# Spreading the inverted softmax sums over the rows: DMAs through memory in place of matmuls, and the normalisation one step later

## The chip, the cores and the metric

The kernel runs on one core of one Trainium2 chip. The metric is device time in microseconds (us): the median of the runs. A profile of one execution stands beside it. The core has TensorE (PE; its weight loads are PEld), VectorE (DVE), ScalarE (ACT), GpSimd (POOL) and SyncE (SP), which here only issues DMAs.

## The reference, cut to what matters

A block of a transformer: cross-attention with a gate, then a mixture of 8 experts with a gate. Only the attention is touched.

```python
x: (4, 512, 512)        # 4 batches of 512 tokens
q = ln(x) @ Wq.T + bq   # 16 heads of 32
k, v = ctx @ Wk.T + bk, ctx @ Wv.T + bv          # 64 context tokens
scores = clip(q k / sqrt(32), -50, 50), masked
probs = softmax(scores)                           # over the 64 context tokens
ctx = einsum(probs, v)                            # 512 tokens x (16 heads x 32)
delta = rs * (ctx @ Wo.T + bo);  x = x + tanh(g) * layernorm(delta) * gamma + beta
x = x + tanh(g2) * experts(ln(x))                 # top 2 of 8
```

The kernel divides by the softmax sum after the product with v: `o_un` is the sum over exp(score) times v, and it is multiplied by the inverse of the sum of its head and token.

## The kernel before, in words

Everything of the attention is kept with features on the partitions and the 512 tokens of a batch along the free axis. The 512 features of a head product are four chunks m (KC = 4) of 128 partitions, and a chunk holds 4 heads a of 32 features. The sums `den` and their inverse `rden` are 16 x 512 (a row per head), so each row must reach the 32 partitions of its head.

Products are made in three fp32r matmuls of a high and a low part (`product3`, L241 to L247; all these matmuls carry line L245). So each operand is split: ACT writes the high part, and DVE or POOL writes the low part, the value minus the high part.

The program is written out by hand for each engine, with semaphores between them. A batch (`batch(b, back, front)`) has 9 steps s = 0 to 8; a step makes the scores of one pair of heads, clips them (DVE), takes their exponential and its two halves (ACT, POOL: `ex_lo`) and multiplies by v (`pv`, one step later). `back` means that the work of the batch before is interleaved: normalising its `o_un`, its output product (`o_product(b - 1, t)` in steps 2 to 5, one tile t of 128 tokens each), its layer norm and update (`update_and_residual`), and the router. `front` means that the next batch is prepared: statistics of its x in steps 1 and 2 (DVE), transposes in step 4, the first half of its q. Batches 1 and 2 have both; batch 0 has no back, batch 3 no front. A tail after batch 3 does the back part of batch 3 alone, and the routing and 37 expert slots follow.

The way of the inverse before: at the end of a batch ACT copies `den` (L946); DVE inverts it (`invert_sums`, L386 to L392) and splits the inverse into `r_hi` and `r_lo`. In step 0 of the next batch PE multiplies both by a selection matrix `bsel` of 16 x 128 for each chunk (`spread`, L1101 to L1111), chunks 0 and 1 behind the q product of chunk 2, and chunks 2 and 3 behind that of chunk 3. DVE multiplies the result in PSUM by `o_un` into `o_n` (two buffers; `normalise`, L394 to L399), ACT copies that to `o_hi` (L899), and POOL subtracts to `o_lo` (L737; in the tail DVE does it, L539). `o_product(n, 0)` waits for each of the four `o_lo` chunks as it comes to it (L1118).

SP issues, in order: for a batch with front the load of the next x into `xs` (L290); with back the stores of the updated rows as they come (L282, L284); then the load of this batch's rows again for the residual, `xr` (L295). The statistics of x wait for `xs` at L346.

Of the kernel before, what the change touches and what calls it, by code (L numbers as in the profile page):

```python
# [41 lines left out]
def flamingo_gated_block(nc, x, ctx_t, mask, w_attn, b_cols, b_rows, gates, gate_t, w_exp, out):  # L42
    st = ExitStack()
    with st:
# [10 lines left out]
        pad_cw = h_dram.rearrange("(n p) d -> n p d", p=P)[NT][:, H:HW]  # L55
        out_rows = out.rearrange("(n p) d -> n p d", p=P)
# [67 lines left out]
        o_n = sb("o_n", [P, 2, S], F32, pa)  # L124
# [76 lines left out]
        def f32(ap):  # L201
            return ap.bitcast(F32)
# [16 lines left out]
        pair_mm, o_ev, den_c, den_r, r_h, r_l, r_mm, o_nd, o_h, o_l = (sem(n) for n in  # L219
            ("pair_product", "context_copied", "sums_copied", "sums_inverted", "inverse_hi", "inverse_lo",  # L220
# [47 lines left out]
        def _(sp):  # L268
# [17 lines left out]
            def batch(b, back, front):  # L286
# [8 lines left out]
                sp.dma_start(xr[:, :, :], x_b[b]).then_inc(rload, 16)  # L295

# [34 lines left out]
        def _(dve):  # L331
# [54 lines left out]
            def invert_sums(n):  # L386
                dve.wait_ge(den_c, n + 1)
                dve.reciprocal(rden[:, :], den[:, :]).then_inc(den_r, 1)  # L388
                dve.wait_ge(den_r, n + 1)
                dve.tensor_scalar(r_hi[:, :], rden[:, :], 1.0, None, ALU.mult).then_inc(r_h, 1)  # L390
                dve.wait_ge(r_h, n + 1)
                dve.tensor_tensor(r_lo[:, :], rden[:, :], f32(r_hi[:, :]), ALU.subtract).then_inc(r_l, 1)  # L392

            def normalise(n, m):  # L394
                dve.wait_ge(r_mm, n * KC + m + 1)
                dve.wait_ge(o_ev, n * KC + m + 1)
                if m >= 2:
                    dve.wait_ge(o_l, n * KC + m - 1)
                dve.tensor_tensor(o_n[:, m % 2, :], bank[m % 2][:, :], o_un[:, m, :], ALU.mult).then_inc(o_nd, 1)  # L399
# [47 lines left out]
            def batch(b, back, front):  # L447
                for s in range(PAIRS + 1):
# [86 lines left out]
            for m in range(KC):  # L535
# [3 lines left out]
                dve.tensor_tensor(o_lo[:, m, :], o_n[:, m % 2, :], f32(o_hi[:, m, :]), ALU.subtract).then_inc(o_l, 1)  # L539
# [165 lines left out]
        def _(pool):  # L705
# [7 lines left out]
            pool.memset(rden[:, :], 1.0).then_inc(setup, 1)  # L713
# [631 lines left out]
```

## Time and profile before

| | us |
|---|---|
| median of 3 runs | 1033.14 |
| lowest and highest | 1032.68, 1034.61 |
| the profiled execution: its span (no other time is listed for it) | 1037.1 |
| PE busy | 929.8 (90%) |
| DVE busy | 471.1 (45%) |
| ACT busy | 366.3 (35%) |
| POOL busy | 261.1 (25%) |
| granted TensorE clock, mean | 0.947 |

The attention with its tail takes the first 290 us or so: setup and projections to about 49, batch 0 to 84, batch 1 to 137, batch 2 to 192, batch 3 to 246, and the tail. A profile row gives the start and duration in us, the engine and the source line, the operation with output and inputs, the shapes and the count. What stands in square brackets is the idle time of the engine just before, and who ended it. The busy share of PE is not PE at its peak, because matmuls overlap: in a chain at full clock a matmul of 512 columns is listed with 0.39 us but starts 0.23 us after the one before.

### The profile page before, as it was taken

Reading aid. Unit: us, or ns where it says so; the run is one execution under the profiler, and the core shown is the slowest. Engines: PE = TensorE matmul, PEld = TensorE weight load, DVE = VectorE, ACT = ScalarE, POOL = GpSimd, SP = SyncE. Lnnn points to the kernel's source line nnn. Section 1 sums busy time; section 2 is a strip of 40 time slices with the busy share of each in tenths; the row PEclk is TensorE's granted clock in tenths of the full one; section 3 lists DMA queues with packets and bytes.
Section 4 is the critical chain, followed back from the end, with each engine's and each line's share of the span. In section 5 each row is a group of like instructions: output and inputs, shape, how many; then the busy total and the mean of one; then the engine's idle time right before and its main releaser. Section 6 shows DMA issues by size and latency. Waiting matters only on the chain.

```text
span 1037.1 us, 14215 instructions
## 1 busy us (share of the span) xinstructions
PE 929.8 (90%) x4201; PEld 723.2 (70%) x4202; DVE 471.1 (45%) x796; ACT 366.3 (35%) x663; POOL 261.1 (25%) x283
## 2 busy tenths in 40 slices
PE   3989999996719999989989989989989998999994
PEld 3756767674517888768868868768868877888883
DVE  5648978786776221451351451621351244226311
ACT  3455554523203222432432442522432253226221
POOL 4034545363231211211211211211211112113111
PEclk9989989997858999999999999999999999999997
DMA  7020121212626211351351361621261235212121
GB/s 289 30 93 0 72 91 51 71 51 77 238 95 253 30 31 30 107 186 30 95 199 28 90 206 26 219 80 22 69 233 20 41 101 182 36 25 30 31 30 20
DMA packets 27824, 93.65 MB, mean 90 GB/s; under 512 B 5408, under 2 KB 5408, under 8 KB 21024
## 3 DMA queue, kind: packets, MB, share of 16 engines
q1 hardware_dynamic: 18528, 72.03, 19.1%
q0 software_dynamic: 8560, 20.35, 10.5%
q10 hardware_dynamic: 720, 1.07, 0.3%
q8 instruction: 8, 0.13, 0.1%
q14 instruction: 8, 0.07, 0.0%
HBM read 74.76 MB, written 18.68 MB: 90 GB/s over the span
## 4 chain that ended last, share of the span: by engine, by line
PE 61%; DMA 16%; issue 9%; DVE 5%; POOL 4%; ACT 2%; POOLq 0%; SPq 0%; DVEq 0%; ACTq 0%
PE bank L245 53%; DMA xg<-h_rows,g_idx 8%; DMA out_rows<-y_sb,s_idx 7%; PE bank L1270 2%; PE bank L1257 2%; DMA xs<-in_x 2%; POOL s_idx L840 1%; PE bank L1143 1%; DVE rden L388 1%; DVE xr L408 1%; ACT y_sb L1045 1%; PE bank L1097 1%; PE bank L1109 1%; PE bank L1130 1%; PE bank L1061 1%
## 5 line engine op out<-in xcount | busy, mean ns | idle before, releaser
L245 PE MATMUL bank<-g_hi,gt_hi 128*128 128x512 f32 x592 | 237.7, 402 | 1.6 <-DVE gt_lo L656 1.6
L245 PE MATMUL bank<-g_hi,gt_lo 128*128 128x512 f32 x592 | 234.7, 396 | 0.0
L245 PE MATMUL bank<-g_lo,gt_hi 128*128 128x512 f32 x592 | 234.5, 396 | 0.0
L686 DVE TENSOR_TENSOR hid<-silu,bank 128x256 f32<-128x256 f32 x148 | 61.5, 420 | 316.6 <-ACT silu L1026 316.5
L1026 ACT ACTIVATE silu<-bank 128x256 f32<-128x256 f32 x148 | 56.7, 383 | 253.2 <-PE bank L245 253.2
L245 PEld LDWEIGHTS bank<-g_hi,gt_hi 128*128 128x128 f32 x592 | 111.7, 189 | 27.6 <-issue 2.0
L245 PEld LDWEIGHTS bank<-g_hi,gt_lo 128*128 128x128 f32 x592 | 111.5, 188 | 27.2
L245 PE MATMUL bank<-dn_hi,hd_hi 128*128 128x512 f32 x296 | 130.2, 440 | 0.0
L245 PEld LDWEIGHTS bank<-g_lo,gt_hi 128*128 128x128 f32 x592 | 111.8, 189 | 25.8
L245 PE MATMUL bank<-dn_lo,hd_hi 128*128 128x512 f32 x296 | 120.0, 405 | 0.0
L245 PE MATMUL bank<-dn_hi,hd_lo 128*128 128x512 f32 x296 | 119.2, 403 | 0.0
L840 POOL COPY s_idx<-slot_idx 128x1 int32 x37 | 20.3, 548 | 357.3 <-ACT y_sb L1045 357.3
L549 DVE TENSOR_TENSOR g_lo<-raw,g_hi 128x2048 fp32r<-128x2048 f32 x32 | 72.4, 2286 | 9.8 <-ACT g_hi L975 9.7
L669 DVE TENSOR_TENSOR hd_lo<-bank,hd_hi 128x256 fp32r<-128x256 f32 x148 | 58.9, 419 | 35.8 <-ACT hd_hi L1009 35.8
L245 PEld LDWEIGHTS bank<-dn_hi,hd_lo 128*128 128x128 f32 x296 | 57.6, 194 | 14.4
L1009 ACT ACTIVATE hd_hi<-bank 128x256 fp32r<-128x256 f32 x148 | 52.5, 384 | 41.4 <-PE bank L1270 41.4
L843 POOL DMA_INDIRECT out_rows<-y_sb,s_idx x37 | 59.3, 1602 | 30.1 <-POOL s_idx L840 30.1
L698 DVE TENSOR_TENSOR gt_lo<-bank,gt_hi 128x512 fp32r<-128x512 f32 x37 | 25.6, 692 | 88.3 <-ACT gt_hi L1038 88.3
L756 POOL TENSOR_TENSOR ex_lo<-ex,ex_hi 128x512 fp32r<-128x512 f32 x32 | 42.0, 1312 | 91.8 <-ACT ex_hi L922 91.7
L975 ACT ACTIVATE g_hi<-raw 128x2048 fp32r<-128x2048 f32 x32 | 61.1, 1910 | 10.5 <-PE bank L245 10.5
L245 PEld LDWEIGHTS bank<-dn_lo,hd_hi 128*128 128x128 f32 x296 | 58.2, 197 | 8.9
L245 PEld LDWEIGHTS bank<-dn_hi,hd_hi 128*128 128x128 f32 x296 | 57.9, 196 | 9.1
(215 smaller groups left out, 1317.4 us busy)
## 6 DMA issues: line engine op xcount, KB each, us to landing
raw<-in_w_exp SPq DMA_DIRECT2D x48, 1024.0 KB, 6.4
raw<-in_w_attn SPq DMA_DIRECT2D x4, 1024.0 KB, 13.6
xs<-in_x SPq DMA_DIRECT2D x4, 1024.0 KB, 6.5
xr<-in_x SPq DMA_DIRECT2D x4, 1024.0 KB, 5.9
out_rows<-xr SPq DMA_DIRECT2D x16, 256.0 KB, 2.0
h_rows<-dh SPq DMA_DIRECT2D x16, 256.0 KB, 2.1
rows<-in_b_rows ACTq DMA_DIRECT2D x1, 1024.0 KB, 13.3
c_raw<-in_ctx_t SPq DMA_DIRECT2D x1, 640.0 KB, 4.2
```

What stands on the lines that cost most here:

```text
L245: mm = eng.matmul(psum, a(k), b(k), start=(first and k == 0 and j == 0), stop=(last and k == n - 1 and j == 2))
L549: dve.tensor_tensor(dst.rearrange("p k n -> p (k n)"), raw[:, p, :], f32(hi.rearrange("p k n -> p (k n)")), ALU.subtract).then_inc(done, 1)
L669: dve.tensor_tensor(hd_lo[:, 2 * p:2 * p + 2, :].rearrange("p k n -> p (k n)"), bank[4 + p % 2][:, 0:256], f32(hd_hi[:, 2 * p:2 * p + 2, : ...
L686: dve.tensor_tensor(hid[:, p, :], silu[:, p, :], bank[p][:, 256:512], ALU.mult).then_inc(hid_done, 1)
L698: dve.tensor_tensor(gt_lo[:, :, :].rearrange("p k n -> p (k n)"), bank[6][:, :], f32(gt_hi[:, :, :].rearrange("p k n -> p (k n)")), ALU.su ...
L756: pool.tensor_tensor(ex_lo[:, s % 2, :], ex[:, s % 2, :], f32(ex_hi[:, s % 2, :]), ALU.subtract).then_inc(e_l, 1)
L840: pool.tensor_copy(s_idx[:, :], slot_idx[:, bass.ds(g, 1)]).then_inc(idx_s, 1)
L843: pool.indirect_dma_start(out=out[:, :], out_offset=bass.IndirectOffsetOnAxis(ap=s_idx[:, 0:1], axis=0), in_=y_sb[:, :], in_offset=None, c ...
L975: act.activation(dst.rearrange("p k n -> p (k n)"), raw[:, p, :], ACT.Copy).then_inc(done, 1)
L1009: act.activation(hd_hi[:, 2 * p:2 * p + 2, :].rearrange("p k n -> p (k n)"), bank[4 + p % 2][:, 0:256], ACT.Copy).then_inc(hd_h, 1)
L1026: act.activation(silu[:, p, :], bank[p][:, 0:256], ACT.Silu).then_inc(silu_done, 1)
L1257: tr = pe.transpose(bank[6][:, k * P:(k + 1) * P], xg[:, k * P:(k + 1) * P], ident[:, :])
```

## The change

The inverse is no longer split and multiplied by `bsel`. A scratch tensor in DRAM, `inverse_rows` (16 x 512), takes `rden` in one store of 32 KB; then four loads, one for each head a of the chunks, read it back, each with a broadcast over 32 partitions and all four chunks m, into a new tile `rbc` (128 x 4 x 512, 1024 KB in all). SP issues all five, after the load of `xr`, and waits for the inverse, for the last `o_lo` of the batch before (which reads `rbc`) and then for its own store. `normalise` multiplies `rbc` by `o_un` in place; `o_hi` and `o_lo` read `rbc` in place of `o_n`. In a batch, the four normalisations, `o_hi` and `o_lo` move from step 0 to step 1. `bsel`, `r_hi`, `r_lo`, `o_n`, `spread`, and the setup of `bsel` are gone.

```diff
+        r_dram = nc.dram_tensor("inverse_rows", [NH, S], F32).ap()
+        r_spread = r_dram.rearrange("(m a) s -> a m s", a=4)
...
-        bsel = sb("bsel", [NH, KC, 4, HD], F32R, pa)
-        r_hi = sb("r_hi", [NH, S], F32R, pa)
-        r_lo = sb("r_lo", [NH, S], F32R, pa)
+        rbc = sb("rbc", [P, KC, S], F32, pa)
-        o_n = sb("o_n", [P, 2, S], F32, pa)
...
 # SP, end of batch
                 sp.dma_start(xr[:, :, :], x_b[b]).then_inc(rload, 16)
+                sp.wait_ge(den_r, b + 1)
+                if back:
+                    sp.wait_ge(o_l, b * KC)
+                sp.dma_start(r_dram, rden[:, :]).then_inc(r_out, 16)
+                sp.wait_ge(r_out, b * 16 + 16)
+                for a in range(4):
+                    sp.dma_start(rbc[a * HD:a * HD + HD, :, :], r_spread[a].partition_broadcast(HD)).then_inc(r_in, 16)
...
 # DVE
             def invert_sums(n):
                 dve.wait_ge(den_c, n + 1)
                 dve.reciprocal(rden[:, :], den[:, :]).then_inc(den_r, 1)
-                dve.wait_ge(den_r, n + 1)
-                dve.tensor_scalar(r_hi[:, :], rden[:, :], 1.0, None, ALU.mult).then_inc(r_h, 1)
-                dve.wait_ge(r_h, n + 1)
-                dve.tensor_tensor(r_lo[:, :], rden[:, :], f32(r_hi[:, :]), ALU.subtract).then_inc(r_l, 1)

             def normalise(n, m):
-                dve.wait_ge(r_mm, n * KC + m + 1)
+                if m == 0:
+                    dve.wait_ge(r_in, n * 64 + 64)
                 dve.wait_ge(o_ev, n * KC + m + 1)
-                if m >= 2:
-                    dve.wait_ge(o_l, n * KC + m - 1)
-                dve.tensor_tensor(o_n[:, m % 2, :], bank[m % 2][:, :], o_un[:, m, :], ALU.mult).then_inc(o_nd, 1)
+                dve.tensor_tensor(rbc[:, m, :], rbc[:, m, :], o_un[:, m, :], ALU.mult).then_inc(o_nd, 1)
...
                     if s == 0:
-                        if back:
-                            normalise(b - 1, 0)
-                            normalise(b - 1, 1)
                         q_low(b, 2)
                         if back:
                             v_low(b)
-                            normalise(b - 1, 2)
-                            normalise(b - 1, 3)
                         q_low(b, 3)
+                    if s == 1 and back:
+                        for m in range(KC):
+                            normalise(b - 1, m)
...
 # POOL: setup of bsel (a memset of rden, an affine select) gone; o_low in step 1
-                    if s == 0 and back:
+                    if s == 1 and back:
                         for m in range(KC):
                             o_low(b - 1, m)
...
 # ACT: the four o_high in step 1, behind the exponential
+                    if s == 1 and back:
+                        for m in range(KC):
+                            o_high(b - 1, m)
...
 # PE, step 0
                         q_product(b, 2)
-                        if back:
-                            spread(b - 1, 0)
-                            spread(b - 1, 1)
                         pe.wait_ge(q_l, b * KC + 2)
                         q_product(b, 3)
-                        if back:
-                            spread(b - 1, 2)
-                            spread(b - 1, 3)
...
 # PE, tail
-            for m in range(KC):
-                spread(NB - 1, m)
```

## Rows read from the trace of the kernel before

**Rows 1.** Stretches: length, busy (count) of PE, PEld, DVE, ACT, POOL, clock, DMA share, GB/s.

```profile
84.00:95.00 11.00, 10.06 (x38) 6.62 (x38) 10.57 (x12) 5.29 (x11) 3.90 (x3) 1.00 0.00 0
...
150.00:165.00 15.00, 15.00 (x50) 10.24 (x49) 12.71 (x28) 7.78 (x12) 11.44 (x11) 0.80 0.05 17
165.00:194.00 29.00, 29.00 (x151) 20.88 (x150) 23.02 (x46) 15.36 (x30) 12.41 (x13) 1.00 0.29 99
...
246.00:249.00 3.00, 0.00 (x0) 0.00 (x0) 3.00 (x1) 0.00 (x0) 2.96 (x3) 0.88 0.00 0
...
255.00:258.00 3.00, 3.00 (x7) 1.90 (x7) 2.71 (x5) 1.41 (x3) 0.00 (x0) 0.50 0.00 0
258.00:261.00 3.00, 3.00 (x13) 2.42 (x12) 1.51 (x3) 0.04 (x1) 0.00 (x0) 0.92 0.86 276
```

**Rows 2.** Timeline, DVE's inversions at the end of batches 0 to 3.

```profile
84.16 3.34 DVE L388 RECIPROCAL rden<-den 16x512 f32<-16x512 f32 x1
...
137.41 3.34 DVE L388 RECIPROCAL rden<-den 16x512 f32<-16x512 f32 x1
...
192.57 3.34 DVE L388 RECIPROCAL rden<-den 16x512 f32<-16x512 f32 x1
...
245.70 3.33 DVE L388 RECIPROCAL rden<-den 16x512 f32<-16x512 f32 x1
```

**Rows 3.** Timeline of the tail, from the inverse to the output product.

```profile
246.03 5.10 POOL L741 TENSOR_TENSOR xr<-xr,rows 128x512 f32<-128x512 f32 x4 [4.25 <-DMA xr<-in_x]
250.05 1.63 DVE L392 TENSOR_TENSOR r_lo<-rden,r_hi 16x512 fp32r<-16x512 f32 x1
251.73 0.79 PE L1109 MATMUL bank<-r_hi,bsel 16*128 16x512 f32 x1 [6.28 <-DVE r_lo L392]
252.98 0.69 DVE L399 TENSOR_TENSOR o_n<-bank,o_un 128x512 f32<-128x512 f32 x1 [1.31 <-PE bank L1109]
253.71 0.63 ACT L899 ACTIVATE o_hi<-o_n 128x512 fp32r<-128x512 f32 x1 [8.12 <-DVE o_n L399]
254.44 0.68 DVE L539 TENSOR_TENSOR o_lo<-o_n,o_hi 128x512 fp32r<-128x512 f32 x1
...
255.73 0.80 PE L245 MATMUL bank<-w_hi,o_hi 128*128 128x512 f32 x1
...
257.40 0.82 SPq L306 DMA_DIRECT2D raw<-in_w_exp  x2
...
260.15 0.75 DVE L415 SCALAR_TENSOR_TENSOR dh<-bank,tg,rows 128x512 f32<-128x512 f32 x1 [1.39 <-PE bank L245]
```

**Rows 4.** Timeline, what follows the first output product in batches 1, 2 and 3.

```profile
100.58 0.50 PE L245 MATMUL bank<-ex_hi,vbd_hi 128*128 128x512 f32 x1
101.79 0.74 DVE L415 SCALAR_TENSOR_TENSOR dh<-bank,tg,rows 128x512 f32<-128x512 f32 x1
...
156.84 0.39 PE L245 MATMUL bank<-ex_hi,vbd_hi 128*128 128x512 f32 x1
157.11 0.75 DVE L415 SCALAR_TENSOR_TENSOR dh<-bank,tg,rows 128x512 f32<-128x512 f32 x1 [1.86 <-PE bank L245]
...
212.03 0.75 DVE L415 SCALAR_TENSOR_TENSOR dh<-bank,tg,rows 128x512 f32<-128x512 f32 x1 [3.81 <-PE bank L245]
```

**Rows 5.** By tile: duration min, median, max in ns, first and last start.

```profile
L1109 PE MATMUL bank<-r_hi,bsel x16: 384/490/790, 88.8 to 254.7; 16*128 16x512 f32 x16
...
L737 POOL TENSOR_TENSOR o_lo<-o_n,o_hi x12: 1278/1314/1362, 92.1 to 206.2; 128x512 fp32r<-128x512 f32 x12
```

**Rows 6.** GB/s of 60 to 70; DMA issues (KB, us to landing) of 128 to 140, 105 to 125.

```profile
GB/s 0 0 0 0 0 0 0 0 0 33 0 0 0 0 0 0 49 164 41 115 270 328 393 418 377 426 410 393 401 279 82 33 16 0 0 0 0 66 0 0
...
xr<-in_x SPq DMA_DIRECT2D x1, 1024.0 KB, 5.8
xs<-in_x SPq DMA_DIRECT2D x1, 1024.0 KB, 7.5
...
out_rows<-xr SPq DMA_DIRECT2D x3, 256.0 KB, 2.0
```

More of the change, by code:

```diff
@@ L218, in flamingo_gated_block @@
             ("scores_product", "scores_clipped", "exp_done", "exp_hi_done", "exp_lo_done"))
-        pair_mm, o_ev, den_c, den_r, r_h, r_l, r_mm, o_nd, o_h, o_l = (sem(n) for n in
-            ("pair_product", "context_copied", "sums_copied", "sums_inverted", "inverse_hi", "inverse_lo",
+        pair_mm, o_ev, den_c, den_r, r_out, r_in, o_nd, o_h, o_l = (sem(n) for n in
+            ("pair_product", "context_copied", "sums_copied", "sums_inverted", "inverse_stored",
              "inverse_spread", "context_normalised", "o_hi_done", "o_lo_done"))
@@ L538, in _ @@
                 dve.wait_ge(o_h, (NB - 1) * KC + m + 1)
-                dve.tensor_tensor(o_lo[:, m, :], o_n[:, m % 2, :], f32(o_hi[:, m, :]), ALU.subtract).then_inc(o_l, 1)
+                dve.tensor_tensor(o_lo[:, m, :], rbc[:, m, :], f32(o_hi[:, m, :]), ALU.subtract).then_inc(o_l, 1)
             for t in range(TT + 2):
@@ L712, in _ @@
                 pool.memset(f32(tile[:]), 0.0).then_inc(setup, 1)
-            pool.memset(rden[:, :], 1.0).then_inc(setup, 1)
-            pool.wait_ge(setup, 9)
+            pool.wait_ge(setup, 8)
             for g in range(2):
                 pool.memset(f32(hsel[g * T:g * T + T, NH - 2 + g:NH - 1 + g]), 1.0).then_inc(setup, 1)
-            pool.affine_select(out=bsel[:, :, :, :], in_=rden[:, :].rearrange("p (m a d) -> p m a d", m=KC, a=4),
-                               compare_op=ALU.is_equal,
-                               fill=0.0, base=0, pattern=[[-4, KC], [-1, 4], [0, HD]],
-                               channel_multiplier=1).then_inc(setup, 1)
             pool.dma_start(out_rows[NT], f32(kbd_hi[:, :, :]).rearrange("p k n -> p (k n)")).then_inc(pad_store, 16)
@@ L736, in o_low @@
                 pool.wait_ge(o_h, n * KC + m + 1)
-                pool.tensor_tensor(o_lo[:, m, :], o_n[:, m % 2, :], f32(o_hi[:, m, :]), ALU.subtract).then_inc(o_l, 1)
+                pool.tensor_tensor(o_lo[:, m, :], rbc[:, m, :], f32(o_hi[:, m, :]), ALU.subtract).then_inc(o_l, 1)
             def add_beta(n, t):
@@ L768, in batch @@
                         add_beta(b - 1, s - 1)
-            pool.wait_ge(setup, 12)
+            pool.wait_ge(setup, 10)
             ln_inverse(0)
@@ L898, in o_high @@
                 act.wait_ge(o_nd, n * KC + m + 1)
-                act.activation(o_hi[:, m, :], o_n[:, m % 2, :], ACT.Copy).then_inc(o_h, 1)
+                act.activation(o_hi[:, m, :], rbc[:, m, :], ACT.Copy).then_inc(o_h, 1)
             def h_copy(n, t, tail=False):
@@ L958, in _ @@
             x_high(0, range(2, KC))
-            act.wait_ge(setup, 12)
+            act.wait_ge(setup, 10)
             act.wait_ge(pad_store, 48)
@@ L1052, in _ @@
             pe.sem_inc(y_ready, 1)
-            pe.wait_ge(setup, 12)
+            pe.wait_ge(setup, 10)
             def x_transposes(n, chunks=range(KC)):
@@ L1099, in pv @@
                 mm.then_inc(pair_mm, 1)
-            def spread(n, m):
-                if m == 0:
-                    pe.wait_ge(r_l, n + 1)
-                    pe.wait_ge(lg_done, n * TT + TT)
-                if m >= 2:
-                    pe.wait_ge(o_nd, n * KC + m - 1)
-                for a, r_ in enumerate((r_hi, r_lo)):
-                    mm = pe.matmul(bank[m % 2][:, :], bsel[:, m, :, :].rearrange("p a d -> p (a d)"), r_[:, :],
-                                   start=(a == 0), stop=(a == 1))
-                mm.then_inc(r_mm, 1)
             def o_product(n, t):
```

6 lines of the change are left out of this document (removed).

## Prediction

> **What bounds the kernel now.** I read first the busy time and clock by stretch, then the timeline around the end of each batch, then the DMA answers. The change sits only in the attention stage and its tail, up to some 290 us; the 37 expert slots behind it keep their work and simply start later or earlier. In the stretch 165 to 194 PE is busy all 29 us at clock 1.00, and in 150 to 165 it is busy all 15 us but at clock 0.80 [rows 1]: inside a batch TensorE sets the pace, and a piece of it runs at 1.2 instead of 2.4 GHz. The start of a batch is different: 84 to 95 has 0.9 us without PE. The reader is to see that whatever delays PE in steps 0 to 2 of a batch is paid nearly in full, because no idle PE time follows in which to win it back. DVE is close behind: it starts `dh` for tile 0 as soon as the first output product is ready, at 101.79, 157.11 and 212.03 us, the last two after 1.9 and 3.8 us of waiting for PE [rows 4]. In batch 3 and in the tail this DVE/POOL chain (scale, statistics, power, update) is the bound, and it starts from the same product. So in all four places one event counts: the end of `o_product(0)`, which needs all four `o_lo` chunks.
>
> The clock: the first spread of the tail starts at 251.73 after 6.28 us of idle, so PE's work ended at 245.45; the clock is 0.88 on the mean of 246 to 249, so it fell near 248.3, some 3 us later; it is 0.50 in 255 to 258 and 0.92 in 258 to 261 [rows 1, 3]. It came back about 6.5 us after work resumed. I use these two as observed, at every gap.
>
> **What is removed.** Per batch 8 matmuls for `spread`, 0.38 to 0.49 us each and overlapping [rows 5], at most 3.1 to 3.9 us of PE, plus PE's wait for `r_lo` in front of them; and the two DVE instructions `r_hi` and `r_lo`. This shortens the time from the inverse to the end of step 0 by about 3 us in batches 1 to 3. It is worth money only if PE is then what ends the wait for `o_product(0)`; below it is not. In the setup, POOL loses one memset and one select; PE starts behind the first split of a weight, long after POOL's setup, so this is nothing, and could only be a gain.
>
> **What is added: a round trip.** The inverse is ready 3.34 us after its start, at 87.50, 140.75, 195.91 and 249.03 [rows 2]. From there: SP wakes and issues, for which I allow 0.17 us without a row. The store of 32 KB: the 256 KB stores land after 2.0 us [rows 6]; most of that can hardly be the bytes, so I take 2.0 for the small one at both ends. Another 0.17 us. Then four loads of 256 KB, each to 32 partitions. Low end: each lands like a lone 256 KB store, 2.0 us, and the last is issued 3 x 0.41 = 1.2 us after the first (two issues in 0.82 us [rows 3]): 3.2 us. Nearest row: the 1024 KB load of x, the same bytes, 5.8 us just before another load [rows 6]. High end: the data part of that load, some 2.6 us near 400 GB/s [rows 6], takes twice as long: 8.4 us. I take the row, 5.8, plus 1.2 us, since the last quarter of the bytes is only issued then: 7.0. The round trip is 0.17 + 2.0 + 0.17 + 7.0 = 9.3 us (ends 5.5 and 10.7).
>
> `rbc` is complete at 96.8, 150.1, 205.2 and 258.3.
>
> **Behind the round trip, in a batch.** The wait stands on DVE at step 1, and queued behind it are the statistics of the next x and the clip of step 2; for that clip wait ACT's exponential, POOL's `ex_lo` and `pv(2)`, and behind the moved `o_hi` and `o_lo` the same two stand in their own queues. All of that is needed only after `o_product(0)` and `pv(1)`, so the product is late first. One normalise (0.69 us) and one `o_hi` (0.63) with hand-overs, as the tail shows (252.98, 253.71, 254.44: 1.46 us for both) [rows 3], take 1.5 us; then POOL does four `o_lo` of 1.31 us [rows 5], 5.3 us; the remaining normalises and `o_hi` pass beside them. The normalise reads two SBUF tiles now, where one came from PSUM. Such a DVE instruction waits for a POOL instruction in progress: `r_lo`, 0.68 us otherwise, took 1.63 beside POOL's `xr` [rows 3]. Two of the four meet this, +0.6 to 1.0 us each; the fourth is then normalised about 3.7 us after the landing, POOL asks for it after 5.4. Cover: 1.7 us minus `o_hi`. The last three matmuls of `o_product(0)` follow, 0.43 us apart (512 columns at 1.2 GHz; 12 of them 5.1 us). Sum: landing + 1.5 + 5.3 + 1.3 = landing + 8.1.
>
> Batch 1: 104.9, where the following matmul group started at 100.58 and DVE at 101.79 [rows 4]: PE +4.3, DVE +3.2. PE idles more than 4 us ahead of the first chunk, so the clock falls here, where it was 1.00 before [rows 1], and comes back near 105; the next 5 matmuls lose up to 1 us. I take +4.5.
> Batch 2: 158.2 against 156.84 and 157.11 [rows 4]: PE +1.4 plus up to 0.9 of slow clock, DVE +1.2. I take +1.8. The 3 us saved on PE and the slow clock of before (0.80 in 150 to 165) are why it is less than in batch 1.
> Batch 3: 213.3 against 212.03 (DVE is the bound): +1.4.
> Tail: landing 258.3, normalise, `o_hi` and DVE's `o_lo` at 0.73 us each, PE starts at 260.6 instead of 255.73 [rows 3]: +4.9. Before, the spread matmuls had run since 251.73 and the clock was back 2.7 us into the output product; now it starts cold and all 12 matmuls of tile 0 take 5.1 us instead of 4.4: +0.8. Together +5.7, all of it on the chain that `dh` at 260.15 begins.
> Sum: 4.5 + 1.8 + 1.4 + 5.7 = 13.4 us.
>
> **What is moved.** The load of the next x is issued behind the four spread loads; before, it went out a step or more ahead of the batch's end. SP waits in order for `den_r` and the store. In batches 1 and 2 DVE wants it right after the fourth normalise, about landing + 3.7. It lands after the spreads: two loads issued one behind the other took 5.8 and 7.5 us [rows 6], so the second comes some 2.6 us behind the first: landing + 2.6. It is hidden with 1.1 us to spare. Were that cover gone, each microsecond would stop DVE's clip of step 2 twice. The load of the residual and the stores of the batch are issued ahead of the wait or well after it: nothing. In the tail the first expert weights wait for the last normalise as before, and are wanted only when the output product is done: nothing. `o_un` is not overwritten before the normalises: its next copy is behind two `pv` steps; nothing, with some microseconds of cover.
>
> **A rule of the Trainium skill.** The row: loads to 128 partitions move near 400 GB/s for 2.6 us [rows 6]; none of this size goes to 32. "SBUF — State Buffer", section "Door 1: The DMA port swizzle", says that the transfer rate depends on how many of 16 ports the partitions reach, that 32 partitions reach 8 of them, and that two transfers at once do not add up. By its 189 GB/s (estimate, that page) the megabyte takes 5.5 us of data instead of 2.6, and the sum would be some 25 us instead of 13. The rule speaks against this change; it is the first rival.
>
> **Rivals.**
> (1) Half rate for the four loads: 8.4 us plus part of the issue lag, 1.4 to 2.4 us more than I took. No row speaks against it; for it, each load touches a quarter of the partitions and all of them read the same 32 KB. It counts in all four places at full: 4 x 1.4 to 4 x 2.4, +19 to +23 us, and x lands late as well, up to 1 us in two batches. Some 1054 us.
> (2) The other side: the quarters overlap, round trip 5.5 us or less. Then `rbc` is there at 93.0, 146.3, 201.4 and 254.5; the clock holds, and `o_product(0)` ends at landing + 7.5: batch 1 0, batch 2 about -2.8, batch 3 -2.9 (the removed matmuls pay at last), tail +1.9: -3.8, 1029 us. It turns at a round trip of about 6.4 us. For it: a lone 256 KB transfer takes 2.0. Against it: 1 MB took 5.8 us.
> (3) The round trip is as I say but x ends the wait of DVE in batches 1 and 2 by 2 us or more, as its one landing of 7.5 us could stretch with the spreads ahead of it: +4, 1050 us.
>
> **How the numbers follow.** The profiled execution spans 1037.1 us and nothing else of it is listed; the median of the runs is 1033.1, 0.4% less. I add the difference to the median: 1033.1 + 13.4 = 1046.5, say 1046. The own range of the forecast is 1040 to 1051 (a round trip of 7.8 to 10.5). Chances: forecast 0.58, rival 1 0.22, rival 2 0.12, rival 3 0.08. The range reaches from 1037 to 1056: it leaves out most of rival 2 and the far part of rival 1. A measurement of this kernel tells 0.2%, 2 us, from no change. Faster by more: 0.08, from rival 2; within: 0.04, its slow edge; slower: 0.88.
>
> **What would show it.** Right: PE idle in front of the first `w_hi,o_hi` matmul in each batch, released by `o_lo`; DVE waiting for the DMA of `rbc` 8 to 10 us after the inverse; half clock at the start of the output product in batch 1 too; `dh` of tile 0 in the tail 17 us after the inverse instead of 11.1 [rows 2, 3]. Wrong: a landing under 6 us after the inverse; PE released by `q_lo` or the probabilities rather than by `o_lo`; a wait of DVE for `xs`; or a later stretch of a batch that gives back what its start lost, which would make the mechanism right and the sum too large.

## The result, and the profile after

The changed kernel takes 1044.61 us (median of 4 runs, 1043.32 to 1047.95) against 1033.88 us for the kernel before on the same chip (4 runs, 1032.68 to 1037.04): ratio 1.0100, 95% interval 1.0065 to 1.0135. Run again unedited later (`changed_again`, 6 runs) it took 1045.84 against 1034.85: ratio 1.0101, interval 1.0068 to 1.0133. It is 10.7 to 11.0 us slower.

First the timeline of the changed kernel around the start of batch 1; it answers to [rows 2, 4]. SPq rows are the issues of DMAs, with the time that SP spent on them.

```profile
79.73 3.34 DVE L394 RECIPROCAL rden<-den 16x512 f32<-16x512 f32 x1
...
83.10 0.34 SPq L298 DMA_DIRECT2D inverse_rows<-rden  x1
...
84.70 1.75 SPq L301 DMA_DIRECT2D rbc<-inverse_rows  x4
...
86.82 0.41 SPq L289 DMA_DIRECT2D xs<-in_x  x1
...
92.85 3.58 DVE L400 TENSOR_TENSOR rbc<-rbc,o_un 128x512 f32<-128x512 f32 x4 [4.00 <-DMA rbc<-inverse_rows]
...
94.28 5.81 POOL L730 TENSOR_TENSOR o_lo<-rbc,o_hi 128x512 fp32r<-128x512 f32 x4 [2.77 <-ACT o_hi L892]
...
95.93 0.79 PE L244 MATMUL bank<-w_hi,o_hi 128*128 128x512 f32 x1 [6.14 <-POOL o_lo L730]
...
101.27 0.74 DVE L416 SCALAR_TENSOR_TENSOR dh<-bank,tg,rows 128x512 f32<-128x512 f32 x1
```

Read it as a chain. The inverse ends at 83.07. The store is issued at once and has landed 1.6 us later, when SP issues the loads; these occupy SP for 1.75 us, and DVE, idle for 4.00 us, starts when they have landed, at 92.85: 8.15 us after the first was issued and 9.78 us after the inverse. POOL then does its four `o_lo` in 5.81 us, 1.45 each, and PE, idle for 6.14 us, waits for them chunk by chunk. The other three places repeat it; each shows the inverse, DVE's first normalise and `dh` of tile 0:

```profile
136.89 3.34 DVE L394 RECIPROCAL rden<-den 16x512 f32<-16x512 f32 x1
...
149.22 3.58 DVE L400 TENSOR_TENSOR rbc<-rbc,o_un 128x512 f32<-128x512 f32 x4 [3.74 <-DMA rbc<-inverse_rows]
...
158.06 0.75 DVE L416 SCALAR_TENSOR_TENSOR dh<-bank,tg,rows 128x512 f32<-128x512 f32 x1 [0.32 <-PE bank L244]
...
193.68 3.34 DVE L394 RECIPROCAL rden<-den 16x512 f32<-16x512 f32 x1
...
205.70 3.58 DVE L400 TENSOR_TENSOR rbc<-rbc,o_un 128x512 f32<-128x512 f32 x4 [3.46 <-DMA rbc<-inverse_rows]
...
214.07 0.75 DVE L416 SCALAR_TENSOR_TENSOR dh<-bank,tg,rows 128x512 f32<-128x512 f32 x1 [4.12 <-PE bank L244]
...
247.73 3.33 DVE L394 RECIPROCAL rden<-den 16x512 f32<-16x512 f32 x1
...
260.01 1.29 DVE L400 TENSOR_TENSOR rbc<-rbc,o_un 128x512 f32<-128x512 f32 x2 [8.95 <-DMA rbc<-inverse_rows]
...
262.15 0.80 PE L244 MATMUL bank<-w_hi,o_hi 128*128 128x512 f32 x1 [14.66 <-DVE o_lo L538]
...
267.38 0.75 DVE L416 SCALAR_TENSOR_TENSOR dh<-bank,tg,rows 128x512 f32<-128x512 f32 x1 [2.09 <-PE bank L244]
```

From the start of an inverse to `dh` of tile 0 these rows give 21.54, 21.17, 20.39 and 19.65 us. Before they were 17.63, 19.70, 19.46 and 14.45 [rows 2 to 4]. The difference is 3.9 + 1.5 + 0.9 + 5.2 = 11.5 us, and the medians differ by 10.7. Within the attention nothing gives it back: from inverse to inverse the batches are longer by 3.9, 1.6 and 0.9 us (57.16, 56.79 and 54.05 against 53.25, 55.16 and 53.13). The two profiled spans differ by less, 1041.6 against 1037.1: the profiled run of before spent 4.4 us more ahead of its first inverse (84.16 against 79.73), and 2.8 us more behind `dh` of the tail (777.0 against 774.2). That last stretch varies from 772.8 to 779.0 us over all the profiles here, so a small gain in the expert stage is neither shown nor excluded.

The stretches from the inverse to `dh` in both kernels show the clock. First the kernel before, batches 1, 2 and 3 (columns as in [rows 1]):

```profile
84.20:101.80 17.60, 16.49 (x63) 10.97 (x63) 17.04 (x27) 8.86 (x17) 9.03 (x8) 1.00 0.00 0
137.40:157.10 19.70, 17.93 (x59) 11.98 (x59) 17.37 (x26) 8.37 (x16) 10.92 (x9) 0.83 0.01 4
192.60:212.00 19.40, 17.86 (x59) 11.99 (x58) 13.96 (x16) 8.35 (x15) 10.20 (x8) 0.82 0.00 0
```

The changed kernel, the same three, then the wait of the tail and the start of its output product:

```profile
79.70:101.30 21.60, 15.08 (x52) 10.07 (x53) 16.52 (x26) 9.01 (x17) 9.57 (x8) 0.84 0.40 99
136.90:158.10 21.20, 15.00 (x51) 10.14 (x50) 16.65 (x25) 8.48 (x16) 9.99 (x8) 0.84 0.36 100
193.70:214.10 20.40, 14.37 (x51) 9.52 (x50) 12.47 (x15) 8.45 (x15) 9.52 (x7) 0.83 0.24 53
249.00:262.00 13.00, 0.00 (x0) 0.00 (x0) 3.95 (x4) 1.23 (x2) 3.44 (x3) 0.53 0.38 84
...
262.00:266.00 4.00, 3.85 (x9) 2.96 (x10) 3.19 (x6) 1.26 (x2) 0.00 (x0) 0.50 0.27 55
```

Batch 1 has gone from 1.00 to 0.84; batches 2 and 3 were at 0.83 and 0.82 already. So batch 1 was the one that ran quickly before (17.63 us, against 19.70 and 19.46), and its loss is the largest for that; after the change all three take 20.4 to 21.5. The fall of the clock in the changed kernel is not itself the price: `fill_wait` below keeps it at 1.00, and batch 1 still takes 21.50. The DMAs of 84 to 105 us answer to [rows 6]:

```profile
rbc<-inverse_rows SPq DMA_DIRECT2D x4, 256.0 KB, 5.3
xs<-in_x SPq DMA_DIRECT2D x1, 1024.0 KB, 8.5
```

The x load, issued at 86.82, landed at 95.3. DVE was normalising until 96.4 and never waited for it.

### The profile page after: what moved, and what is told of

The parts are those of the page before. It is cut to its first block, busy times and chain, and to the rows that moved or that the text cites. A ratio compares the mean times of both kernels' runs of the same rounds, so it can differ in the third digit from the quotient of the medians.

```text
span 1041.6 us, 14150 instructions
## 1 busy us (share of the span) xinstructions
PE 912.7 (88%) x4169; PEld 712.8 (68%) x4170; DVE 465.2 (45%) x788; ACT 366.3 (35%) x663; POOL 261.1 (25%) x281
## 4 chain that ended last, share of the span: by engine, by line
PE 56%; DMA 18%; issue 11%; DVE 5%; POOL 5%; ACT 3%; POOLq 0%; SPq 0%; DVEq 0%; ACTq 0%
PE bank L244 49%; DMA xg<-h_rows,g_idx 8%; DMA out_rows<-y_sb,s_idx 7%; PE bank L1240 2%; PE bank L1227 2%; DMA xs<-in_x 2%; POOL s_idx L833 1%; POOL o_lo L730 1%; DMA rbc<-inverse_rows 1%; DVE xr L409 1%; ACT y_sb L1035 1%; POOL ex_lo L749 1%; PE bank L1121 1%; DVE st L424 1%; DVE rden L394 1%
```

## The experiments

The table sets beside each other, for every kernel, the median, its ratio to the kernel before with the interval, and the time from the start of the inverse to `dh` of tile 0 in batches 1, 2, 3 and the tail (from the timeline of its one profile). The kernel before had medians of 1033.58 to 1034.85 in the four sets of runs beside these.

| kernel | us | ratio (95%) | b1 | b2 | b3 | tail |
|---|---|---|---|---|---|---|
| before | 1033.88 | | 17.63 | 19.70 | 19.46 | 14.45 |
| changed | 1044.61 | 1.0100 (1.0065 to 1.0135) | 21.54 | 21.17 | 20.39 | 19.65 |
| changed_again | 1045.84 | 1.0101 (1.0068 to 1.0133) | 22.12 | 21.16 | 20.49 | 19.65 |
| store_twice | 1051.09 | 1.0154 (1.0119 to 1.0189) | 22.13 | 22.15 | 22.23 | 20.69 |
| two_queues | 1048.45 | 1.0134 (1.0097 to 1.0172) | 21.32 | 22.28 | 21.63 | 17.73 |
| tail_matmul_2 | 1042.59 | 1.0072 (1.0049 to 1.0094) | 22.23 | 21.61 | 20.44 | 15.47 |
| move_only | 1036.95 | 1.0031 (1.0005 to 1.0057) | 20.09 | 20.23 | 19.28 | 14.18 |
| fill_wait | 1046.59 | 1.0111 (1.0074 to 1.0147) | 21.50 | 20.71 | 20.53 | 18.36 |
| eight_back | 1048.67 | 1.0143 (1.0114 to 1.0171) | 21.75 | 21.31 | 21.81 | 19.61 |
| before_warm_tail | 1029.71 | 0.9956 (0.9930 to 0.9983) | 17.62 | 17.79 | 19.46 | 13.66 |
| warm_again | 1034.17 | 1.0001 (0.9974 to 1.0028) | 17.66 | 19.71 | 19.47 | 13.63 |
| warm_only | 1032.41 | 0.9983 (0.9954 to 1.0012) | 18.83 | 17.77 | 17.59 | 15.32 |
| pool_wait_only | 1035.42 | 1.0013 (0.9986 to 1.0040) | 17.65 | 19.69 | 19.46 | 14.20 |

**What sets the time of the loads: probe.** The kernel before, with transfers one after another at its very end, when nothing else runs (one execution; the edit is shown shortened).

```diff
+            sp.dma_start(p_dram, raw[0:NH, 0, 0:S])     # 32 KB store, then wait
+            for a in range(4): quarter(sp, a, spread_src, pr_s[1])   # as in the change
+            for a in range(4): quarter(sp, a, rows_src, pr_s[2])     # distinct rows of x
+            sp.dma_start(t4, x_b[0])                                 # 128 partitions at once
+            sp.dma_start(t4, p_spread[0].partition_broadcast(P))     # 128 partitions, the same 4 rows
```

> The kernel before, and behind its end, when nothing else runs, SP issues transfers one group after the other, each awaited, all with 1024 KB in or out of one tile except where said: a 32 KB store of 16 rows; four quarters to 32 partitions each from the 16 rows just stored (the change's loads); four quarters to the same partitions from distinct rows of x; one load of x to 128 partitions; one load to 128 partitions in which all partitions read the same 4 rows; the four quarters from the 16 rows in the order 0, 2, 1, 3; a single quarter; the store again. Theory A (a transfer to 32 partitions has half the rate, by the partitions it reaches): the quarters of x take as long as those of the stored rows, 7.2 us from the first issue, at about 220 GB/s; both loads to 128 partitions take 5.5 us at up to 400 GB/s; the order 0, 2, 1, 3 gains little. Theory B (the many reads of the same 32 KB in memory are what is slow): the quarters of x take about 5.5 to 6 us, and the load of 128 partitions that read the same 4 rows is slow, 7 us or more. Theory C (four issues instead of one): the quarters of x take 6 to 6.5 us and both loads to 128 partitions 5.5. The store takes 1.6 us in every theory.

Issues in the timeline of `probe`; each group waits for the landing of the one before, so the distance to the next row is the time to landing (the last `x5` are two groups: four quarters in the order 0, 2, 1, 3, and at 1062.48 a lone one):

```profile
1026.44 0.34 SPq L335 DMA_DIRECT2D probe_rows<-raw  x1
...
1028.04 1.76 SPq L340 DMA_DIRECT2D raw<-probe_rows  x4
...
1035.29 1.75 SPq L340 DMA_DIRECT2D raw<-in_x  x4
...
1042.14 0.40 SPq L353 DMA_DIRECT2D raw<-in_x  x1
...
1047.31 0.39 SPq L355 DMA_DIRECT2D raw<-probe_rows  x1
...
1055.56 7.22 SPq L340 DMA_DIRECT2D raw<-probe_rows  x5
```

The store 1.60 us; four quarters from the stored rows 7.25; four quarters of distinct rows 6.85; the same megabyte in one load to 128 partitions 5.17; one load to 128 partitions that all read the same four rows 8.25. In the order 0, 2, 1, 3 the quarters take 6.9. So it is the quarters that cost, 1.7 us over a whole load, and rereading the same rows adds 0.4 to them. Issuing in four pieces is not the cause: a lone quarter lands after 3.4 us, and the last is issued 1.3 us behind the first, which would make 4.7. And one load that reads the same rows for all partitions is the slowest of the four. Theory A is right for the quarters and wrong for that load, theory B the other way round. The rate in 40 equal slices of 1026 to 1060 us shows it from another side:

```profile
GB/s 0 39 0 82 195 282 222 227 166 60 0 0 164 306 193 222 205 145 0 0 87 219 400 402 125 0 125 171 130 176 108 171 176 152 24 14 176 299 236 248
```

After the store (39) come the four transfers, with zeros between: the quarters of stored rows at some 220 GB/s, those of x at some 210, the load to 128 partitions at 400, the one of repeated rows at 108 to 176. The Trainium skill, "SBUF — State Buffer", section "Door 1: The DMA port swizzle", has 32 partitions at 189 GB/s and 128 at 328, both for a whole transfer of 1 MiB, with limits of some 218 and 436 for large ones. The trace agrees with the limits (220 and 210, 400). The prediction took the 189 for the rate of the data alone; at the 220 measured the megabyte is 4.8 us of data and not 5.5.

That transfers to different partitions don't add up, as the prediction has it from the same page, is not borne out by these traces as it stands. With a queue of SP and one of ACT, to partitions 0 to 63 and 64 to 127, the loads of `two_queues` (below) reached 377 GB/s over their best microsecond in the tail, the first row here, and 361 in batch 3. On one queue the best microsecond of four quarters is 318, in the probe's quarters of x, the second row:

```profile
259.70:260.70 1.00, 0.00 (x0) 0.00 (x0) 0.00 (x0) 0.00 (x0) 0.00 (x0) 0.50 1.09 377
...
1036.80:1037.80 1.00, 0.00 (x0) 0.00 (x0) 0.00 (x0) 0.00 (x0) 0.00 (x0) 0.50 1.05 318
```

**Is the round trip on the path: store_twice.** A second store of the same 32 KB between the first and the loads.

```diff
-                sp.wait_ge(r_out, b * 16 + 16)
+                sp.wait_ge(r_out, b * 32 + 16)
+                sp.dma_start(r_dram, rden[:, :]).then_inc(r_out, 16)
+                sp.wait_ge(r_out, b * 32 + 32)
```

> The changed kernel, but SP stores the inverse twice, waiting in between, so that each of the four round trips is 1.6 to 1.8 us longer and nothing else changes. Theory of the prediction (every microsecond of the round trip is paid in all four places, about one for one): 4 x 1.7 = +6 to +7.5 us, 1051 to 1052. Rival (later steps of a batch give back what its start lost, so that only the tail pays): +2 us, 1046 to 1047.

The second store took 1.57 to 1.60 us each time (in batch 2 issued at 147.24, the loads at 148.82). The kernel took 1051.09 us, 6.5 more than the changed one, and 6.0 to 6.2 when each is set against the kernel before in its own set of runs; 4 x 1.58 is 6.3, and the rival said 2. The profiles say less, and not the same in each place: `dh` is 0.6, 1.0, 1.8 and 1.0 us later after the inverse than in the changed kernel, and 5.0 us from the first inverse to `dh` of the tail (4.4 against `changed_again`, whose batch 1 is as long as this one). So most of a longer round trip is paid, in the batches as in the tail; that it is paid in full in every place is not shown.

**Can the round trip be shortened: two_queues.** Two of the four loads are issued by ACT at the end of its batch.

```diff
-                for a in range(4):
+                for a in (0, 1):
...
+            def spread_loads(b):                     # ACT, last in its batch
+                act.wait_ge(r_out, b * 16 + 16)
+                for a in (2, 3):
+                    act.dma_start(rbc[a * HD:a * HD + HD, :, :], ...).then_inc(r_in, 16)
```

> The changed kernel, but the loads of quarters 2 and 3 (partitions 64 to 127) are issued by ACT on its own queue, behind its last work of the batch, while SP issues quarters 0 and 1 (partitions 0 to 63). Theory A (half the SBUF side is used at a time): with both halves in flight at once the spread lands about 1.5 to 2.5 us earlier, so each of the four places gives back that much, 6 to 8 us in all: 1037 to 1039 us. Theory B (the reads of the same 32 KB are slow) or a limit that concurrent transfers share: the landing stays within 0.5 us, and the time within 2 us of the changed kernel, or a little above it for ACT's wait at the start of a batch.

Neither theory was right: the loads landed 6.0 to 6.9 us after the first issue in place of 7.1 to 8.2, the tail gained 1.9 us by it, and the whole became slower. The batches gained nothing, as batch 2 of `two_queues` shows:

```profile
146.65 1.26 POOL L749 TENSOR_TENSOR ex_lo<-ex,ex_hi 128x512 fp32r<-128x512 f32 x1 [13.94 <-ACT ex_hi L920]
...
150.07 4.66 DVE L400 TENSOR_TENSOR rbc<-rbc,o_un 128x512 f32<-128x512 f32 x4 [0.25 <-DMA rbc<-inverse_rows]
...
151.22 1.27 POOL L749 TENSOR_TENSOR ex_lo<-ex,ex_hi 128x512 fp32r<-128x512 f32 x1 [3.31 <-ACT ex_hi L920]
```

The loads are there 0.8 us sooner after the inverse (138.53 to 150.07, 11.5 us, against 12.3), and DVE waits 0.25 us for them instead of 3.74: it has only just got there. ACT's wait for the store holds up what is queued behind it, its exponential, and so POOL's `ex_lo`, PE and DVE's clip. `ex_lo` of the next step now falls on the normalises, which take 4.66 us for four in place of 3.58, and POOL comes to its first `o_lo` 2.4 us after the first normalise starts (152.46) instead of 1.4. A wait had changed its place. By the profile the batches are 2.7 us longer in sum, inverse to inverse, and the tail is 1.9 shorter. The medians differ by 3.8, but the six runs fall in two groups, 1044.7 to 1046.1 and 1050.8 to 1051.9, and the profile is of the fastest; what the second group does more is open.

**How much belongs to the tail: tail_matmul_2.** The changed kernel with the matmul way for batch 3 alone (inverse split in two, `spread` and `normalise` from PSUM in the tail; no store and loads). The two halves lie in `ex_hi` and `ex_lo`: as tiles of their own (`tail_matmul`) they do not fit in SBUF beside `rbc`, the last tile needing 8192 bytes a partition where 6240 are left.

```diff
+                if not front:
+                    return                            # SP: no round trip in batch 3
...
+                if tail:
+                    dve.tensor_scalar(ex_hi[0:NH, 0, :], rden[:, :], 1.0, None, ALU.mult).then_inc(r_h, 1)
...
+                    dve.tensor_tensor(ex_lo[0:NH, 0, :], rden[:, :], f32(ex_hi[0:NH, 0, :]), ALU.subtract).then_inc(r_l, 1)
...
+            for m in range(KC):
+                spread(NB - 1, m)                     # PE, tail
```

> The changed kernel, but batch 3's inverse is spread by the matmuls of before (with bsel, and the two halves kept in ex_hi and ex_lo), in the tail only; batches 0 to 2 keep the DMAs. Theory of the prediction (each round trip is paid where it stands): the tail gets back what it lost, 5 us on the profile between the inverse and the first dh, so 1039 to 1040 us; what is left above the kernel before, 6 us, is the three batches. Rival (the tail's loss is hidden by the load and split of the first expert weights, and the expert stage only starts when those are there): within 1.5 us of the changed kernel.

Median 1042.59, 8.2 us above before, where the changed kernel is 10.7 to 11.0. The tail's time is 15.47 against 19.65 in the profile: 4.2 us there, 2.5 to 2.8 by the medians, whose intervals overlap; 5 was expected, and at most 1.5 by the rival. PE starts the output product 9.87 us after the inverse began, as early as before (10.03). What is not won back, 1.0 us against the 14.45 of before, is the clock: from that matmul to `dh` it is 5.60 us here at 0.50 nearly throughout, and 4.42 before. So the tail's share of the loss is a quarter of it by the medians and up to 5.2 of 11.7 us by the profiles; the larger part lies in the three batches.

**How much belongs to the move: move_only.** The kernel before with `spread`, `normalise`, `o_hi` and `o_lo` in step 1, in PE's, DVE's, ACT's and POOL's order; no DMA.

```diff
-                        if back:
-                            spread(b - 1, 0)
-                            spread(b - 1, 1)
...
+                    if s == 1 and back:
+                        spread(b - 1, 0)
+                        spread(b - 1, 1)
...
+                    if s == 1 and back:
+                        for m in range(KC):
+                            normalise(b - 1, m)
```

> The kernel before with the move alone: spread stays on PE, but stands in step 1 (chunks 0 and 1 behind the scores, 2 and 3 behind pv(0)), and the normalisations, o_hi and o_lo stand in step 1 too. Theory 1 (the round trip alone makes the loss): the move costs little, 1033 to 1036 us; o_lo is still the last thing before o_product(0), now some 2 to 3 us later after the inverse than before, but PE reaches the step earlier. Theory 2 (a good part of the loss in the batches is the move, which puts four o_lo of POOL, 5.3 us, in one row in front of o_product(0)): 1038 us or more.

1036.95 against 1034.35: +2.6 us, interval 0.5 to 5.9, between the two theories. The profile has +2.5 in batch 1, +0.5 in batch 2, -0.2 in batch 3 and -0.3 in the tail, +2.5 in sum: nearly all of it in batch 1. There it is the clock. First PE's output product in batch 1 of the kernel before, then the same of `move_only`, and two stretches of `move_only`:

```profile
97.49 0.50 PE L245 MATMUL bank<-w_hi,o_hi 128*128 128x512 f32 x1
97.83 0.39 PE L245 MATMUL bank<-w_lo,o_hi 128*128 128x512 f32 x1
...
94.15 0.76 PE L245 MATMUL bank<-w_hi,o_hi 128*128 128x512 f32 x1 [0.28 <-POOL o_lo L735]
94.71 0.63 PE L245 MATMUL bank<-w_lo,o_hi 128*128 128x512 f32 x1
...
88.00:91.30 3.30, 3.15 (x12) 1.81 (x11) 3.23 (x5) 1.17 (x2) 0.47 (x1) 1.00 0.00 0
94.30:97.30 3.00, 3.00 (x7) 1.96 (x8) 2.44 (x5) 1.26 (x2) 2.69 (x3) 0.50 0.00 0
```

The product starts 13.62 us after the inverse began, against 13.33 before, but its matmuls follow each other every 0.43 us instead of 0.23, and twelve of them make up the 2.5 us. The clock had fallen near 91.3, though by the profile PE had been idle for only 0.2 us since 80.5; why it fell is open. Batches 2 and 3 are at 0.83 and 0.82 with the move as they are without it, and change by 0.5 and -0.2. So the place in the order costs little by itself. The 2.5 us is no part of the changed kernel's loss in batch 1 either, since with its clock held at 1.00 (`fill_wait`, next) that batch is as long.

**Is it the cold clock: fill_wait.** The changed kernel with 26 matmuls of 512 columns put into PE's wait in step 1, and 62 into that of the tail; their result is read by nobody.

```diff
+                    if s == 1 and back:
+                        fill(b - 1, 26)
...
+            fill(NB - 1, 62)
```

> The changed kernel with matmuls that nobody reads in PE's waits: 26 of 512 columns behind pv(0) of batches 1 to 3, and 62 in front of the tail's output product (6 and 14 us at full clock, about the waits that the profile shows). Everything else is unchanged. Theory 1 (part of the loss is the slow clock after each wait): the output product starts at full clock; in a batch the last three matmuls save 0.6 us and the next group up to 1, in the tail 2 us or so: 1040 to 1042. Theory 2 (the POOL and DMA chain is all): within 1 us of the changed kernel, 1044 to 1046; or slower, if the matmuls run at the slow clock and push the output product back.

The clock stayed at full speed, as the stretches 140 to 160 and 262 to 270 of `fill_wait` show:

```profile
140.00:160.00 20.00, 18.43 (x74) 13.23 (x74) 15.84 (x24) 8.23 (x15) 9.19 (x7) 1.00 0.39 107
...
262.00:270.00 8.00, 7.63 (x32) 5.56 (x31) 5.86 (x10) 2.50 (x4) 0.00 (x0) 1.00 0.29 88
```

The product starts as early as without the filling (16.16 us after the inverse began in batch 1, against 16.20). Only the tail gained clearly, 1.3 us, and batch 2 by 0.5; the median is 1046.59, no better than the changed kernel, as theory 2 has it. In a batch the product is fed by POOL, a chunk every 1.45 us, which is longer than its three matmuls take at either level (3 x 0.43 = 1.3). So in the batches of the changed kernel the slow clock is a companion of the wait and hardly a cost of its own. In the kernel before, where PE itself is what `dh` waits for, it is one: 1.9 us a batch, as `before_warm_tail` shows below.

**Were the removed matmuls worth nothing: eight_back.** The changed kernel with eight matmuls where the spreads stood, beside `changed_again`.

```diff
                         q_product(b, 2)
+                        if back:
+                            fill(b - 1, 4)
...
                         q_product(b, 3)
+                        if back:
+                            fill(b - 1, 4)
```

> The changed kernel with eight matmuls of 128x512 put back into step 0 of each batch with a back part (four behind each of the two q products, where the spreads stood), on operands that are already there; their result is read by nobody, so the output is the same. The prediction held that the eight removed matmuls were worth nothing, since the end of o_product(0) hangs on the round trip and not on PE. That theory expects 1043 to 1046 us, within 2 us of the changed kernel run beside it, PE's idle time ahead of the first output product shorter by about 3 us (from 6.1 us to about 3 in batch 1) and the time from the inverse to dh of tile 0 the same to 0.5 us. The rival, that the removed matmuls gave back up to 3 us of PE per batch and so hid a part of the round trip's price, expects 3 x 1 to 3 x 3 us more, 1048 to 1054 us.

> The changed kernel itself, unedited, beside eight_back on the same chip, so that the two can be compared at 0.2%. Both theories expect 1043 to 1046 us; and they expect of its profile that the time from the inverse to dh of tile 0 repeats to 0.5 us in all four places (21.5, 21.2, 20.4, 19.7), while the head up to the first inverse varies by up to some us with the granted clock.

1048.67 against 1045.84: +2.8 us, more than the 2 of the first theory, just under the 3 where the rival begins, and with intervals that overlap. PE's idle time ahead of the product in batch 1 is 4.16 us, 2.0 shorter than in the changed kernel. Inverse to inverse its batches are 57.39, 56.94 and 56.19 us long, those of `changed_again` 57.60, 56.81 and 54.19: all of it in batch 3. There the normalises of `eight_back`, and POOL's `ex_lo` of step 1:

```profile
207.56 1.26 POOL L749 TENSOR_TENSOR ex_lo<-ex,ex_hi 128x512 fp32r<-128x512 f32 x1 [5.02 <-ACT ex_hi L915]
...
207.88 4.38 DVE L400 TENSOR_TENSOR rbc<-rbc,o_un 128x512 f32<-128x512 f32 x4 [1.72 <-DMA rbc<-inverse_rows]
```

and those of `changed_again`:

```profile
207.43 1.26 POOL L749 TENSOR_TENSOR ex_lo<-ex,ex_hi 128x512 fp32r<-128x512 f32 x1 [3.31 <-ACT ex_hi L915]
...
209.56 3.58 DVE L400 TENSOR_TENSOR rbc<-rbc,o_un 128x512 f32<-128x512 f32 x4 [3.54 <-DMA rbc<-inverse_rows]
```

With the matmuls the step runs later, `ex_lo` falls on the first normalise, and the four take 0.8 us longer. PE starts the product at 211.85 in the one and 212.74 in the other; the stretch of 3 us that begins 2.2 us after that is at 0.50 in `eight_back`,

```profile
214.00:217.00 3.00, 3.00 (x8) 2.08 (x7) 0.00 (x0) 0.24 (x1) 3.00 (x3) 0.50 0.00 0
```

and at 0.75 in `changed_again`, so the clock came back later as well:

```profile
215.00:218.00 3.00, 3.00 (x11) 2.08 (x10) 0.06 (x1) 0.14 (x1) 3.00 (x3) 0.75 0.00 0
```

Batches 1 and 2 show the first effect (4.33 and 4.10 for four) and not the loss, so in this profile the removed matmuls were worth nothing in two batches and 2 us in one. That is also what the clock alone moves a batch of the kernel before by, without any edit ahead of it (next experiment). Their value is small, and that it is nothing is neither upheld nor refuted.

**A faster version of before: before_warm_tail.** The kernel before, its tail filled with 18 matmuls ahead of the spreads, and POOL's additions of the tail held back until `r_lo` is done.

```diff
+            pool.wait_ge(r_l, NB)
...
+            for _ in range(18):
+                pe.matmul(bank[0][:, :], w_hi[:, 1, 0, 0:P], w_hi[:, 1, 1, :], start=True, stop=True)
```

> The kernel before with two changes in its tail alone: POOL adds beta to the residual only when r_lo is done (DVE's r_hi and r_lo took 2.6 us beside it, 1.1 elsewhere), and PE runs 18 matmuls that nobody reads (4.1 us) while it waits for r_lo. If the tail is a chain from the inverse to dh, as the prediction says, it gains 1.5 us from the first and up to 2.5 from the clock: 1030 to 1032 us, faster than both kernels. Rival (the expert stage waits for its weights): no change.

It came out 4.6 us under the kernel before, though the tail is only 0.8 us shorter. So it was run again with its two halves by themselves:

> The kernel before with the 18 idle-filling matmuls of 128x512 ahead of the tail's spreads, and nothing else (before_warm_tail without POOL's wait). Theory: the clock was what made the tail of before_warm_tail shorter; then this kernel keeps most of its gain: 2 to 4 us under the kernel before, 1030 to 1033 us, the inverse to dh of tile 0 some 13.9 to 14.2 us against 14.45. Rival: POOL's wait did it (r_lo no longer runs beside POOL), and the fill alone is within 1 us of the kernel before.

> The kernel before with POOL's four residual additions of the tail held back until r_lo is done, and nothing else (before_warm_tail without the matmuls). Theory: r_lo takes 0.7 in place of 1.6 us, so the inverse to dh of tile 0 shrinks by 0.9 us at most, and the clock still falls; 0 to 1 us under the kernel before. Rival: it gives the 4 to 5 us of before_warm_tail by itself, 1029 to 1031 us.

> before_warm_tail again, unedited, beside its two halves. Expected to repeat: a ratio of 0.993 to 0.998 to the kernel before. If it comes out at 0.998 or more, the gain measured first was mostly chance of the clock elsewhere; the rows of the tail promise only 0.8 us (13.66 against 14.45).

`warm_again` stands at 1.0001 (0.9974 to 1.0028), and neither half shows a difference. The tail's time repeats (13.66, 13.63), the gain of the whole does not; no version here is shown to beat the kernel before. The table says where the first gain lay: batch 2 took 17.79 us there, 19.71 in `warm_again`. Its stretch in `before_warm_tail`, which answers to the 0.83 of before:

```profile
132.90:150.70 17.80, 15.99 (x62) 10.52 (x60) 17.32 (x27) 8.38 (x15) 9.08 (x8) 1.00 0.02 8
```

The same instructions at 1.00 instead of 0.83 are 1.9 us shorter. Against such a batch 2 the changed kernel's 21.17 is a loss of 3.4 us and not of 1.5: how the loss divides over the batches hangs on the clock that the kernel before happened to have. `warm_only` has short ones in batches 2 and 3 (17.77, 17.59); its 18.83 in batch 1 is not explained.

## Why the prediction was right, point by point

It said 1046 us, 1037 to 1056, slower with 0.88, and the kernel takes 1044.6.

**The event.** Right. PE's first `w_hi,o_hi` matmul is released by POOL's (in the tail DVE's) `o_lo` in all four places, and DVE by the DMA of `rbc` before that; `store_twice` shows that most of any lengthening is paid.

**The round trip, 9.3 us.** Right in sum: 9.8, 9.0, 8.7 and 8.95 us from the end of the inverse to the first normalise. Its parts were off both ways, the store 1.6 in place of 2.0, the loads 7.1 to 8.2 in place of 7.0, and that they cancel is luck. The reason given for the 7.0 (a load of the same bytes plus the lag of issuing) was wrong. The probe shows that the quarters move at about half the rate of a whole load, and that a lone whole load takes 5.2 us and not the 5.8 of the row: the mechanism of rival 1, at the price of the forecast. Rival 1 went wrong by doubling the data time and keeping all the rest.

**Landing to the end of the first product, 8.1 us.** Measured 8.3 in batch 1 (92.85 to the last matmul's end at 101.1). POOL's `o_lo` took 1.45 us each where 1.31 was taken; the clock, back at 99.1, made the last matmuls shorter.

**The four terms.** Batch 1: 4.5, measured 3.9. Batch 2: 1.8, measured 1.6. Batch 3: 1.4, measured 0.9. Tail: 5.7, measured 5.2. Sum 13.4, measured 11.7 (187.65 us from the first inverse to `dh` of the tail, against 175.99) and 10.7 by the medians. Each is 0.2 to 0.6 too large. In batch 1 the forecast went by PE: its next group of matmuls does start 4.8 us later after the inverse (100.96 in this profile), but `dh` and the whole batch are 3.9 later, which is DVE's figure; the prediction had 3.2 for that. The clock, taken to return 6.5 us after work resumed, returned 3.2, 5.0, 3.1 and 4.5 us after PE's first `o_product` matmul, by the distances of the matmuls; the up to 1 us put down for it in batch 1 should have been near nothing, as `fill_wait` shows. In the tail PE starts 4.4 us later and not 4.9, most of which is the shorter round trip (8.95 for 9.3), and the 0.8 for the slow clock is there as forecast: 5.23 us from PE's first matmul to `dh`, against 4.42.

**The removed matmuls, nothing.** Not settled: put back, they cost 2.8 us by the medians (`eight_back`), with intervals that overlap, and in the profile all of it in one batch. The prediction did not price the move by itself either. `move_only` shows 2.6 us for it, but as a clock that falls in batch 1, which the changed kernel's time there does not depend on; and since the forecast set the whole new path against the old one, the sum held what the move costs there.

**The moved load of x.** Right: 1.1 us to spare was said, and it landed 1.1 us before the last normalise ended. Rival 3 did not occur. Rival 2 would have needed a round trip under 6.4 us; the best seen, with two queues in the tail, is 7.7.

**The median as base.** The forecast was added to the median and not to the profiled 1037.1, which was right: that run's surplus lay in its head and behind the tail, where no instruction that counts was changed. The head up to the first inverse is 79.6 to 84.2 us in the profiles of the kernel before and its variants and 79.7 to 84.5 in those of the changed one, so the setup that was taken out is worth nothing that can be seen, as forecast.

## What to carry to other kernels

To take matmuls off a busy TensorE pays only where TensorE ends the wait. That is how the chain here reads; what the removed matmuls were worth was too small to tell. What replaced them shows plainly: 3.95 us from the end of the inverse to the first normalise (the tail, 249.03 to 252.98 [rows 2, 3]) became 8.95. Price such a trip as store, landing, loads to the partitions they really touch, and all that queues behind the landing, and look at every engine's order: a wait taken from SP to ACT came back on POOL and DVE.

## What the runs showed of the hardware

- A megabyte from memory into SBUF: 5.2 us to 128 partitions from distinct rows, 6.9 in four loads to 32 partitions each, 7.25 the same with each load reading four rows 32 times, 8.25 in one load to 128 partitions that all read the same four rows. That the last is slower than the quarters was not expected; why was not tried.
- The same four loads on two queues reached 377 GB/s over their best microsecond (tail of `two_queues`), on one queue at most 318, and landed 6.0 us after the first issue in place of 7.3.
- A store of 32 KB lands 1.6 us after its issue, in every kernel that has one.
- After a pause of TensorE the clock returned 3.0 to 5.0 us after work resumed in the changed kernel, more than 5 us after it in batch 3 of `eight_back` (0.50 still in 214 to 217, with PE at work from 211.85), and 9.7 us after it in the tail of `tail_matmul_2` (at work from 257.37, by the distances of the matmuls). It can also fall without a pause: in batch 1 of `move_only` near 91.3, with PE busy for 10.6 of the 10.8 us before. The same instructions of batch 2 took 17.8 or 19.7 us in kernels that do not differ up to there. Where a ratio within 0.5% rests on such a phase, only a repeat tells: the interval 0.9930 to 0.9983 of one set of runs became 0.9974 to 1.0028 in the next.
